# A graph layer with a mixture of experts on one core: expert results stored whole at their list rows, and gathered from there block by block

## The chip, the cores and the metric

The kernel runs on one core of a Trainium2 chip. The metric is the device time of one launch in microseconds; smaller is better. Three runs of the kernel before gave 1312.43, 1315.35 and 1317.46 us, with a median of 1315.35 us.

## The reference

There are 6250 nodes with 256 features, padded to 49 blocks of 128 nodes, and 100,000 edges. First a graph layer, then a layer of 8 experts of which each node uses two:

```python
x = x + gnn(layernorm(x)); x = x + ffn(layernorm(x))
# gnn: out = feat @ W_self + (segment_sum(feat[src], dst) / max(deg, 1)) @ W_neigh + b
# ffn: xn = layernorm(x) * gamma + beta;  logits = xn @ Wr + br
#      two best experts of a node, w = softmax(their logits)
#      h = gelu(xn @ W1[e] + b1[e]);  y_e = h @ W2[e] + b2[e]     (W1: 256x512, W2: 512x256)
#      y = y + y_e * w_full[..., e]
```

All of it is float32. The edges come sorted by `dst`.

## The kernel before, in words

**Slots.** Everything is laid out in slots `t`, numbered from 0 on. `plan` gives each step of each piece of work a slot, and every engine's program is a loop over the slots. The engines meet at semaphores alone.

**Edges.** In each of the slots 0 to 195 one group of 512 edges is worked off. GpSimd gathers their source rows from `feature_table` with four indirect DMAs (`gather`, L660) into `ring`, which holds four groups. GpSimd may therefore be at most about three groups ahead of TensorE. VectorE builds one-hot matrices (L1220), TensorE multiplies (`group`, L927, 8 rows of matmul in the trace per slot), and VectorE adds the sums to `agg` (L1274).

**Blocks.** As the edges of a block of 128 nodes are done, the block (called n, counted from the last block of nodes) goes through turns, products, normalization and the router. A routed block gets, for each node, two places in the lists of its experts (`slots`), and GpSimd scatters its rows twice into `expert_rows` (`scatter_rows`, L668).

**Dense blocks.** Blocks in `DENSE_BLOCKS`, nine of them (and the last block, 48), are not routed. They run through all eight experts, one *unit* per expert and block (`early_in`, hidden L1003 and result L1037), and VectorE adds each expert's share to `agg` (L1448, L1452). This fills the time before there are lists.

**Tiles.** Routed rows are worked off in 85 tiles of 128 rows of one expert's list. SyncE loads rows and weights (`load_rows`, `load_w1_of`), TensorE does hidden (L1003) and result (L1029), VectorE adds the bias and weighs (`weighted`, L1426, L1428). Then GpSimd puts the tile's rows with one indirect DMA into `node_rows`, which has two rows per node (`put_rows`, L679); the row number travels as an extra column of the list row. A tile is a unit too.

**Merges.** For each routed block SyncE loads the two rows of each node with one plain DMA (`load_pair`, L487), the two are added, the block's `x1` is added (L1409), and SyncE stores the block (`store_merged`, L493). 22 merges are done in slots 136 to 181, with two buffers, both additions on VectorE. They may start there because `merge_claim` proves from the counts that certain early blocks have all been handed out. The other 17 come at the end, behind the last tile. There GpSimd does the first addition (L686), ten buffers are used, and the second additions stand among the eight units of the last dense block on VectorE, three behind each `dense_sum`.

If a claim fails, all engines run the whole second half again, by a slow general path (`again`).

Of the kernel before, what the change touches and what calls it, by code (L numbers as in the profile page):

```python
# [6 lines left out]
P = 128  # L7
F32 = mybir.dt.float32
# [13 lines left out]
XP = 6  # L22
XR = 9
XW = 3
XY = 6
CONSTS = 20
EMPTY = 18
RAW = 4
DENSE_BLOCKS = (0, 3, 6, 9, 15, 21, 27, 33, 47)
DENSE_GAP = (1.25, 2.3)  # L30
MERGE_CLAIMS = ((28, 8), (32, 16), (36, 20), (40, 24), (44, 28))
MERGE_BUFFERS = 10
# [14 lines left out]
              "weigh": (5, 2), "add": (9, 5)}  # L47
# [5 lines left out]
def plan(NB, NG, NE):  # L53

# [78 lines left out]
def build(nc, x, src, dst, w_self, w_neigh, b_gnn, gamma, beta, w_r, b_r, w1, b1, w2, b2, out):  # L133
# [17 lines left out]
    merge_buffer = [i % 2 if at is not None else i % MERGE_BUFFERS for i, (n, c, at) in enumerate(merges)]  # L151
# [16 lines left out]
    node_rows = nc.dram_tensor("node_rows", [2 * NP + 3 * P, D], F32, kind="Internal").ap()  # L168
# [7 lines left out]
    with ExitStack() as ctx:  # L176
# [37 lines left out]
        node_i = sb("node_i", [P, NB, 2], I32)  # L214
# [6 lines left out]
        empty_row = sb("empty_row", [P, 3, R])  # L221
# [23 lines left out]
        slot_i = [sb(f"slot_i{s}", [P, 2], I32) for s in range(XP)]  # L245
# [43 lines left out]
        pair = sb("pair", [P, 2 * D])  # L289
        ring_flat = ring[:, :, :].rearrange("p a b -> p (a b)")  # L290
        merge_b = [dst_i[:, DK * P:DK * P + 2 * D].bitcast(F32), pair[:, :]]
        merge_b += [ring_flat[:, k * 2 * D:(k + 1) * 2 * D] for k in range(MERGE_BUFFERS - 2)]
        snap = sb("snap", [1, len(MERGE_CLAIMS), NE])
        late = sb("late", [1, len(MERGE_CLAIMS) + 1])
# [7 lines left out]
        small_in, dst_in, src_in, w2_in, b_in = (sem(n) for n in ("small_in", "dst_in", "src_in", "w2_in", "b_in"))  # L302
# [93 lines left out]
        merge_io = [(s, 16) for s in x_in] + [(sem(f"merge_io{k}"), 0) for k in range(MERGE_BUFFERS - len(x_in))]  # L396
# [38 lines left out]

        def dense_in(t):

            return [e for e in range(NE) if DENSE + e == t]
# [4 lines left out]
        def _(sp):  # L443
# [25 lines left out]
            sp.dma_start(out[NP:NP + P, :], empty_row[:, 0, 0:D]).then_inc(trash_out, 16)  # L469
# [67 lines left out]
            for t in range(END):  # L537
# [13 lines left out]
                for i in merges_in(t, 2):  # L551
                    load_pair(i)
# [1088 lines left out]
```

## Time and profile before

| | us |
|---|---|
| median of three runs | 1315.35 |
| time of the profiled execution | 1316.61 |
| its span in the trace | 1314.6 |
| TensorE matmul busy | 1155.8 |
| VectorE busy | 879.9 |
| ScalarE busy | 424.9 |
| GpSimd busy | 960.6 |

The mean granted clock of TensorE was 0.968. Times in the trace count from the start of the span. "Busy" for a GpSimd indirect DMA is the time in which GpSimd makes its descriptors; the transfer comes after. A short idle time stands ahead of each of these instructions, and the rows list it apart as idle released by "issue". A slot ends with its eight L927 matmuls, so slot borders can be read from them: slot 54 ends at 357 us, slot 136 at 884, slot 180 at 1177, slot 195 at 1264.

### The profile page before, as it was taken

To read this page: it belongs to the slowest core of one execution; us is meant where nothing else is said; L and a number is where in the kernel's file an instruction comes from. 1 tells how busy PE (TensorE), PEld (TensorE's weight loads), DVE (VectorE), ACT (ScalarE), POOL (GpSimd) and SP (SyncE) were. 2 spreads that over 40 slices of the span, in tenths; PEclk is the share of its full clock that TensorE was granted. 3 is DMA by queue.
4 is the path that set the end of the run, shared out by engine and by line. 5 is a ranking of instruction groups with operands and counts; after the bars stand their busy time and mean duration, and the time that the engine had idled before them with its cause. 6 is when DMAs were issued, how large, how long until landed. Compare 5 with 4: busy or idle time off the path is not lost.

```text
span 1314.6 us, 22817 instructions
## 1 busy us (share of the span) xinstructions
PE 1155.8 (88%) x6764; PEld 1030.2 (78%) x6765; DVE 879.9 (67%) x2835; ACT 424.9 (32%) x795; POOL 960.6 (73%) x1039
## 2 busy tenths in 40 slices
PE   0269999999988989999998999999888897999978
PEld 0248888888977879898897988988777795888867
DVE  6946666677677576877666677786587775664536
ACT  5503333323324333343342333343233331311121
POOL 6577777777767777777777777777777777777752
PEclk9978999999989999999998999999899998999989
DMA  9887765656655666666666756667557677677657
GB/s 334 263 259 226 221 194 178 189 168 197 206 165 171 200 193 209 189 210 205 197 221 185 214 183 191 204 212 245 178 168 228 224 235 237 224 236 219 222 165 233
DMA packets 154938, 276.16 MB, mean 210 GB/s; under 512 B 26464, under 2 KB 76896, under 8 KB 154688
## 3 DMA queue, kind: packets, MB, share of 16 engines
q1 hardware_dynamic: 103792, 142.94, 33.8%
q0 software_dynamic: 45456, 124.27, 30.9%
q10 hardware_dynamic: 5568, 7.47, 1.8%
q8 instruction: 59, 0.97, 0.3%
q14 instruction: 63, 0.52, 0.1%
HBM read 236.72 MB, written 37.86 MB: 209 GB/s over the span
## 4 chain that ended last, share of the span: by engine, by line
PE 73%; DVE 16%; issue 5%; DMA 2%; ACT 2%; POOL 1%; DVEq 1%; SPq 0%; ACTq 0%; POOLq 0%
PE bank L927 22%; PE bank L1003 19%; PE bank L1029 11%; PE bank L1037 9%; PE bank L915 3%; PE bank L956 3%; PE bank L958 3%; DVE heap L1417 2%; DVE agg L1274 2%; ACT heap L766 1%; DMA heap<-in_x 1%; PE bank L973 1%; DVE onehot L1220 1%; POOL ring L660 1%; PE bank L1053 1%
## 5 line engine op out<-in xcount | busy, mean ns | idle before, releaser
L660 POOL DMA_INDIRECT ring<-feature_table,src_sb x768 | 748.6, 975 | 252.5 <-issue 220.6
L927 PE MATMUL bank<-ring,onehot 128*128 128x257 f32 x1568 | 394.8, 396 | 84.8 <-DVE onehot L1220 52.6
L927 PEld LDWEIGHTS bank<-ring,onehot 128*128 128x128 f32 x1568 | 307.7, 199 | 140.4 <-issue 82.6
L1417 DVE TENSOR_TENSOR heap<-bank,b_sb 128x512 f32<-128x512 f32 x157 | 108.4, 691 | 224.7 <-PE bank L1003 83.5
L828 ACT ACTIVATE heap<-heap 128x512 f32<-128x512 f32 x157 | 98.9, 630 | 429.8 <-DVE heap L1417 429.8
L1029 PE MATMUL bank<-heap 128*128 x680 | 170.5, 395 | 18.4 <-DVE inside L1426 6.2
L1003 PE MATMUL bank<-row_t,heap 128*128 128x128 f32 x1360 | 166.8, 276 | 1.8 <-DVE heap L1417 1.8
L1003 PEld LDWEIGHTS bank<-row_t,heap 128*128 128x128 f32 x1360 | 161.1, 193 | 3.7 <-issue 2.6
L1029 PEld LDWEIGHTS bank<-heap 128*128 128x128 f32 x680 | 127.8, 196 | 36.9 <-issue 21.1
L1037 PE MATMUL bank<-heap 128*128 128x256 f32 x576 | 142.5, 391 | 15.8 <-DVE agg L1452 8.8
L1003 PE MATMUL bank<-dst_i,heap 128*128 128x128 f32 x1152 | 141.6, 276 | 0.6 <-DVE heap L1417 0.6
L1003 PEld LDWEIGHTS bank<-dst_i,heap 128*128 128x128 f32 x1152 | 137.9, 193 | 3.9 <-issue 1.6
L1274 DVE SCALAR_TENSOR_TENSOR agg<-bank,in_first,agg 128x257 f32 x196 | 94.2, 480 | 69.2 <-PE bank L927 44.2
L1220 DVE TENSOR_TENSOR onehot<-iota,target 128x512 f32<-128x512 f32 x196 | 134.4, 686 | 6.1 <-DVE xf L1291 5.0
L1037 PEld LDWEIGHTS bank<-heap 128*128 128x128 f32 x576 | 106.9, 193 | 30.6 <-issue 17.7
L821 ACT ACTIVATE row_t<-bank,gb_sb 128x128 f32<-128x128 f32 x170 | 68.4, 454 | 118.3 <-PE bank L915 118.2
L668 POOL DMA_INDIRECT expert_rows<-rows,slot_i x78 | 80.6, 1034 | 23.8 <-issue 23.8
L1274 DVE SCALAR_TENSOR_TENSOR agg<-bank,in_second,agg 128x257 f32 x196 | 93.2, 475 | 0.0
L788 ACT ACT_TABLE_LOAD x47 | 60.3, 1283 | 0.8
L956 PE MATMUL bank<-wn_sb,sums_t 128*128 128x256 f32 x196 | 53.8, 398 | 7.2 <-DVE logits L1324 6.4
L828 ACT ACT_TABLE_LOAD x46 | 59.0, 1283 | 0.8
L806 ACT ACTIVATE normal_t<-bank,gb_sb 128x128 f32<-128x128 f32 x80 | 32.1, 451 | 77.1 <-PE bank L915 77.1
(179 smaller groups left out, 1241.7 us busy)
## 6 DMA issues: line engine op xcount, KB each, us to landing
heap<-in_w SPq DMA_DIRECT2D x314, 256.0 KB
ring<-feature_table,src_sb POOLq DMA_INDIRECT x768
row<-expert_rows SPq DMA_DIRECT2D x85, 129.0 KB, 4.1
xf<-in_x SPq DMA_DIRECT2D x49, 128.0 KB
ff<-feature_table SPq DMA_DIRECT2D x49, 128.0 KB
feature_table<-heap SPq DMA_DIRECT2D x6, 896.0 KB, 5.7
heap<-in_w SPq DMA_DIRECT2D x4, 1024.0 KB, 5.7
heap<-in_w ACTq DMA_DIRECT2D x16, 256.0 KB
```

The lines of the kernel that those rows point to most:

```text
L660: pool.indirect_dma_start(ring[:, q * GT + i, 0:D], None, x if t < RAW else table, bass.IndirectOffsetOnAxis(src_sb[:, k:k + 1], 0)).then_ ...
L668: pool.indirect_dma_start(rows_tab, bass.IndirectOffsetOnAxis(slot_i[s][:, c:c + 1], 0), rows[s][:, c, :], None).then_inc(S.scattered[s], 16)
L821: last = act.activation(row_t[s][:, k, :], turned_b[:, k * P:(k + 1) * P], ACT.Identity, bias=gb_sb[:, 1, k:k + 1], scale=gb_sb[:, 0, k:k ...
L828: act.activation(hid[s], hid[s], ACT.Gelu).then_inc(S.gelu, 1)
L927: last = pe.matmul(bank[t % 2][:, 0:D + 1], onehot[:, q, i, :], ring[:, q * GT + i, :], start=(i == 0), stop=(i == GT - 1))
L956: pe.matmul(product_b[:, D:2 * D], t[:, k, :], wn_sb[:, k, :], start=(k == 0), stop=(k == DK - 1))
L1003: last = pe.matmul(hidden_b[:, c * P:(c + 1) * P], w1_of[w][:, k, c * P:(c + 1) * P], turned[:, k, :], start=(k == 0), stop=(k == DK - 1))
L1029: last = pe.matmul(result_b[:, 0:D], hid[s][:, k, :], w2_sb[:, k, bass.ds(e, 1), :].rearrange("p o d -> p (o d)"), start=(k == 0), stop=(k ...
L1037: last = pe.matmul(result_b[:, 0:D], hid[unit_of_dense[u] % 2][:, k, :], w2_sb[:, k, u % NE, :], start=(k == 0), stop=(k == HK - 1))
L1220: dve.tensor_tensor(onehot[:, q, :, :], iota[:, :].unsqueeze(1).broadcast_to([P, GT, P]), target[:, g * GT:(g + 1) * GT].unsqueeze(2).broa ...
L1274: last = dve.scalar_tensor_tensor(out=a, in0=bank[t % 2][:, 0:D + 1], scalar=mask[:, g:g + 1], in1=a, op0=ALU.mult, op1=ALU.add)
L1417: dve.tensor_tensor(hid[S.slot(u, 2)], hidden_b[:, :].rearrange("p (k t) -> p k t", k=HK), b1_sb[:, bass.ds(e, 1), :].rearrange("p o k -> ...
```

## The change

Three things are changed together.

1. **Results are stored whole.** `put_rows` on GpSimd is gone. SyncE stores the 128 rows of a tile with one plain DMA in `expert_out`, at the same place that its rows had in the lists (`store_rows`), two slots behind the weighing. The place of every node's two rows is now kept for all blocks (`slots_of`).
2. **Merges gather.** GpSimd gathers the rows of each node of a block with two indirect DMAs from `expert_out` into the two halves of a merge buffer (`take_rows`). It does so in the same slot in which VectorE adds both halves and `x1` (`add_rows`), with three buffers in the stage and eight at the end. SyncE no longer loads pairs, and GpSimd no longer adds.
3. **Seven dense blocks.** They are 0, 3, 6, 9, 18, 27 and 47, not 0, 3, 6, 9, 15, 21, 27, 33 and 47. There are then 56 dense units, not 72, and 89 tiles, not 85. 41 blocks are merged, not 39: 23 in slots 136 to 180 and 18 at the end.

An expert's share of the table is now 2176 rows on the planned path; if an expert has more than 2048 rows (`share_claim`), the slow path runs. SyncE also fills the whole of `expert_out` with zeros, in 68 DMAs of 256 rows of 1 KB each (17.8 MB), two in each of the slots 10 to 43.

```diff
-CONSTS = 20
+CONSTS = 16
+SHARE = 17 * P
-DENSE_BLOCKS = (0, 3, 6, 9, 15, 21, 27, 33, 47)
+DENSE_BLOCKS = (0, 3, 6, 9, 18, 27, 47)
-MERGE_CLAIMS = ((28, 8), (32, 16), (36, 20), (40, 24), (44, 28))
-MERGE_BUFFERS = 10
+MERGE_CLAIMS = ((28, 12), (32, 16), (36, 20), (40, 24), (44, 28))
+MERGE_BUFFERS = 8
+MERGE_SEMS = 4
+STAGE_BUFFERS = 3
...
-              "weigh": (5, 2), "add": (9, 5)}
+              "weigh": (5, 2), "store": (7, 4), "add": (9, 5)}
...
+    CAP = 3 * SHARE
+    FILLS = NE * SHARE // (2 * P)
...
-            def load_pair(i):
-                n, c, at = merges[i]
-                k = merge_buffer[i]
-                if k >= 2:
-                    sp.wait_ge(summed, NG)
-                io, base = merge_io[k]
-                sp.wait_ge(io, base + 32 * merge_use[i])
-                tiles_put(hold, main, lists[c][1])
-                b = NB - 1 - n
-                sp.dma_start(merge_b[k], node_rows[2 * P * b:2 * P * (b + 1), :].rearrange("(p c) d -> p (c d)", c=2)).then_inc(io, 16)
...
+            def store_rows(S, j):
+                if S.planned:
+                    tiles_put(hold, S, max(j - 1, 0))
+                else:
+                    hold(S.y_put[0], 16 * j)
+                hold(S.y_set, j + 1)
+                if S.planned and j == 0:
+                    sp.wait_ge(trash_out, 16 * (FILLS + EMPTY + 1))
+                at, = load_values(mybir.EngineType.SP, list_i[0:1, bass.ds(j, 1), 1], NE * CAP + (EMPTY - 1) * P, **unchecked)
+                sp.dma_start(expert_out[bass.ds(at, P), :], y_out[S.slot(j, XY)][:, :]).then_inc(S.y_put[S.slot(j, 2)], 16)
...
+                for i in range(FILLS):
+                    if t == 2 * HK + 2 + i // 2:
+                        two = expert_out[2 * P * i:2 * P * (i + 1), :].rearrange("(p c) d -> p c d", c=2)
+                        sp.dma_start(two, empty_row[:, 0:D].unsqueeze(1).broadcast_to([P, 2, D])).then_inc(trash_out, 16)
+                for j in tiles_in(t, "store"):
+                    store_rows(main, j)
                 for i in merges_in(t, -1):
                     store_merged(i)
-                for i in merges_in(t, 2):
-                    load_pair(i)
...
-            def put_rows(S, j):
-                if S.planned:
-                    tiles_put(hold, S, max(j - 1, 0))
-                else:
-                    hold(S.y_put[0], 16 * j)
-                hold(S.y_set, j + 1)
-                pool.indirect_dma_start(node_rows, bass.IndirectOffsetOnAxis(row[S.slot(j, XR)][:, D + 1:R].bitcast(I32), 0),
-                                        y_out[S.slot(j, XY)][:, :], None).then_inc(S.y_put[S.slot(j, 2)], 16)
-
-            def add_pair(i):
+            def take_rows(i):
+                n, of_list, at = merges[i]
                 k = merge_buffer[i]
-                io, base = merge_io[k]
-                pool.wait_ge(io, base + 32 * merge_use[i] + 16)
-                pool.tensor_tensor(merge_b[k][:, 0:D], merge_b[k][:, 0:D], merge_b[k][:, D:2 * D], ALU.add).then_inc(halved, 1)
+                if k >= STAGE_BUFFERS:
+                    pool.wait_ge(summed, NG)
+                pool.wait_ge(x_in[k], 16 * (merge_use[i] + 1))
+                pool.wait_ge(taken[i % MERGE_SEMS], 32 * (i // MERGE_SEMS))
+                tiles_put(hold, main, lists[of_list][1])
+                for c in range(2):
+                    pool.indirect_dma_start(merge_b[k][:, c * D:(c + 1) * D], None, expert_out[0:NE * SHARE, :],
+                                            bass.IndirectOffsetOnAxis(slots_at(main, n)[:, c:c + 1], 0)).then_inc(taken[i % MERGE_SEMS], 16)
...
                 for n in routed_in(t, "scatter"):
                     scatter_rows(main, n)
-                for j in tiles_in(t, "add"):
-                    put_rows(main, j)
+                for i in merges_in(t):
+                    take_rows(i)
             for i in range(STAGE_MERGES, len(merges)):
-                add_pair(i)
+                take_rows(i)
...
+            def add_rows(i):
                 k = merge_buffer[i]
-                io, base = merge_io[k]
-                dve.wait_ge(io, base + 32 * merge_use[i] + 16)
-                dve.tensor_tensor(merge_b[k][:, 0:D], merge_b[k][:, 0:D], merge_b[k][:, D:2 * D], ALU.add).then_inc(halved, 1)
+                m = merge_b[k]
+                after = linker(halved, i, 1)
+                dve.wait_ge(taken[i % MERGE_SEMS], 32 * (i // MERGE_SEMS + 1))
+                after(dve.tensor_tensor(m[:, 0:D], m[:, 0:D], m[:, D:2 * D], ALU.add))
+                dve.tensor_tensor(m[:, 0:D], m[:, 0:D], x1_of(main, merges[i][0]), ALU.add).then_inc(merged, 1)
```

The order of instructions shows where this lands. On GpSimd (POOL), from the first tiles on, in the kernel before; `node_rows` is where a put goes, `expert_rows` where a scatter goes, `ring` where a gather goes (x4 is one slot):

```order
L660 DMA ring<-feature_table,src_sb 128x256 x12
L668 DMA expert_rows<-rows2,slot_i2 53504x258 x2
L679 DMA node_rows<-inside,row1 12928x256
L660 DMA ring<-feature_table,src_sb 128x256 x8
L679 DMA node_rows<-inside,row2 12928x256
L660 DMA ring<-feature_table,src_sb 128x256 x4
L668 DMA expert_rows<-rows3,slot_i3 53504x258 x2
L679 DMA node_rows<-y_out3,row3 12928x256
```

And the same stretch of GpSimd after the change:

```order
L674 DMA ring<-feature_table,src_sb 128x256 x16
L682 DMA expert_rows<-rows2,slots_of 54528x257 x2
L674 DMA ring<-feature_table,src_sb 128x256 x12
L682 DMA expert_rows<-rows3,slots_of 54528x257 x2
L674 DMA ring<-feature_table,src_sb 128x256 x12
L682 DMA expert_rows<-rows4,slots_of 54528x257 x2
```

The puts are gone from between the gathers. Of the 85 puts, 38 stood in slots before 136, 35 in slots 136 to 180, 8 in slots 181 to 195 and 4 behind the last gather. In their place stand pairs of gathers from `expert_out`, 23 pairs in slots 136 to 180. The end of GpSimd's program in the kernel before, from the last gather of edges (here a put, then four, then the first additions of pairs):

```order
L660 DMA ring<-feature_table,src_sb 128x256 x4
L679 DMA node_rows<-y_out3,row0 12928x256
L679 DMA node_rows<-y_out4,row1 12928x256
L679 DMA node_rows<-y_out5,row2 12928x256
L679 DMA node_rows<-inside,row3 12928x256
L686 TENSOR_TENSOR ring<-ring 128x256 x8
L686 TENSOR_TENSOR dst_i<-dst_i 128x256
L686 TENSOR_TENSOR pair<-pair 128x256
L686 TENSOR_TENSOR ring<-ring 128x256 x7
```

And the end after the change, from the last pair in the stage on:

```order
L695 DMA pair0<-expert_out,slots_of 128x256 x2
L674 DMA ring<-feature_table,src_sb 128x256 x60
L695 DMA ring<-expert_out,slots_of 128x256 x2
L695 DMA dst_i<-expert_out,slots_of 128x256 x2
L695 DMA pair0<-expert_out,slots_of 128x256 x2
L695 DMA pair1<-expert_out,slots_of 128x256 x2
L695 DMA ring<-expert_out,slots_of 128x256 x10
L695 DMA dst_i<-expert_out,slots_of 128x256 x2
L695 DMA pair0<-expert_out,slots_of 128x256 x2
L695 DMA pair1<-expert_out,slots_of 128x256 x2
L695 DMA ring<-expert_out,slots_of 128x256 x10
L695 DMA dst_i<-expert_out,slots_of 128x256 x2
```

The last 15 slots now hold gathers of edges alone on GpSimd, and 36 gathers of result rows stand behind them, all of which wait for the last tile's store. On SyncE, in the first of the slots 10 to 43, after the change (`in_w1` are expert weights; the rows with `expert_out` are new):

```order
L562 DMA expert_rows<-empty_row 128x257
L566 DMA expert_out<-empty_row 256x1x256 x2
L517 DMA heap<-in_w1 128x512 x2
L562 DMA expert_rows<-empty_row 128x257
L566 DMA expert_out<-empty_row 256x1x256 x2
L488 DMA xf1<-in_x 128x256
L489 DMA ff1<-feature_table 128x256
```

The two zero fills of a slot stand ahead of the slot's loads of nodes and weights in the same queue.

## Rows read from the trace of the kernel before

**Rows 1.** The page, parts 1 and 4: engines busy; chain that ended last.
```profile
PE 1155.8 (88%) x6764; PEld 1030.2 (78%) x6765; DVE 879.9 (67%) x2835; ACT 424.9 (32%) x795; POOL 960.6 (73%) x1039
...
PE 73%; DVE 16%; issue 5%; DMA 2%; ACT 2%; POOL 1%; DVEq 1%; SPq 0%; ACTq 0%; POOLq 0%
```

**Rows 2.** Windows: start:end length, busy and count by engine, PEclk, DMA share, GB/s.
```profile
53.00:357.00 304.00, 270.99 (x1530) 239.94 (x1530) 205.57 (x663) 88.73 (x156) 226.20 (x232) 0.96 0.66 205
357.00:884.00 527.00, 500.14 (x3004) 450.70 (x3003) 371.69 (x1252) 189.63 (x350) 400.61 (x407) 0.98 0.63 197
884.00:1177.00 293.00, 259.69 (x1515) 229.73 (x1514) 193.25 (x616) 87.42 (x172) 222.14 (x225) 0.97 0.69 220
1177.00:1266.00 89.00, 83.80 (x503) 73.79 (x501) 43.74 (x90) 16.71 (x33) 66.27 (x68) 1.00 0.67 213
90.00:100.00 10.00, 4.26 (x11) 3.44 (x12) 1.66 (x4) 0.03 (x1) 7.57 (x9) 0.58 1.03 361
```

**Rows 3.** Groups of GpSimd instructions, window 357:884: busy, mean ns, idle before.
```profile
L660 POOL DMA_INDIRECT ring<-feature_table,src_sb x326 | 316.5, 971 | 102.0 <-issue 95.4 <-PE bank L927 3.8 <-DVE rows L1345 2.6
L668 POOL DMA_INDIRECT expert_rows<-rows,slot_i x42 | 44.3, 1055 | 12.8 <-issue 12.8
L679 POOL DMA_INDIRECT node_rows<-inside,row x21 | 21.6, 1030 | 6.4 <-issue 6.1 <-DVE rows L1345 0.3
L679 POOL DMA_INDIRECT node_rows<-y_out,row x18 | 18.3, 1019 | 5.5 <-issue 5.5
```

**Rows 4.** The same groups of GpSimd, window 884:1177.
```profile
L660 POOL DMA_INDIRECT ring<-feature_table,src_sb x171 | 168.0, 983 | 52.5 <-issue 47.2 <-PE bank L927 1.9 <-DVE inside L1428 1.2
L668 POOL DMA_INDIRECT expert_rows<-rows,slot_i x20 | 20.0, 998 | 6.1 <-issue 6.1
L679 POOL DMA_INDIRECT node_rows<-y_out,row x18 | 18.2, 1014 | 6.6 <-issue 5.2 <-DVE y_out L1428 1.4
L679 POOL DMA_INDIRECT node_rows<-inside,row x16 | 16.7, 1046 | 5.8 <-issue 4.3 <-DVE inside L1428 1.2 <-DVE y_out L1428 0.3
```

**Rows 5.** Waits of TensorE, window 1177:1266: engine, line, releaser, us, times, longest.
```profile
PE bank L927 <- issue: 5.1, 6, 2.0
```

**Rows 6.** The chain that ended last, from 1177: start, length, what.
```profile
1182.50 1.79 PE bank L1003 x16
1184.28 1.73 PE bank L1029 x8
...
1264.12 1.76 PE bank L1029 x8
```

**Rows 7.** Timeline of TensorE at slot 136: start, length, instructions.
```profile
882.35 1.90 PE L927 MATMUL bank<-ring,onehot 128*128 128x257 f32 x8
```

**Rows 8.** Timeline of GpSimd: the last gather of slot 136.
```profile
867.69 0.95 POOL L660 DMA_INDIRECT ring<-feature_table,src_sb  x1 [0.30 <-issue]
```

**Rows 9.** The page, part 3: packets, MB, share of 16 engines' span.
```profile
q1 hardware_dynamic: 103792, 142.94, 33.8%
```

**Rows 10.** Timeline, 86:101: the group of slot 10 and the gathers around.
```profile
88.34 0.95 POOL L660 DMA_INDIRECT ring<-feature_table,src_sb  x1 [0.30 <-issue]
95.74 3.77 PE L927 MATMUL bank<-ring,onehot 128*128 128x257 f32 x8 [6.86 <-issue]
```

**Rows 11.** Puts (L679) in the whole trace: the row on landing.
```profile
DMA to landing us min/median/max: 2.4/2.5/5.5
```

**Rows 12.** Timeline, 1262:1275: last tile weighed, put, and first pair load.
```profile
1266.57 0.35 DVE L1428 TENSOR_SCALAR inside<-inside,row 128x256 f32<-128x256 f32 x1
1267.73 0.97 POOL L679 DMA_INDIRECT node_rows<-inside,row  x1 [2.52 <-DVE inside L1428]
1270.29 3.27 SPq L487 DMA_DIRECT2D ring<-node_rows  x7
```

**Rows 13.** Timeline, 1303:1316: the last steps of all.
```profile
1306.19 1.01 DVE L1409 TENSOR_TENSOR ring<-ring,agg 128x256 f32<-128x256 f32 x2
1311.14 0.33 SPq L583 DMA_DIRECT2D out<-agg  x1
```

More of the change, by code:

```diff
@@ L150, in build @@
     UNITS = EARLY + NJ
-    merge_buffer = [i % 2 if at is not None else i % MERGE_BUFFERS for i, (n, c, at) in enumerate(merges)]
+    merge_buffer = [i % STAGE_BUFFERS if at is not None else i % MERGE_BUFFERS for i, (n, c, at) in enumerate(merges)]
     merge_use = [merge_buffer[:i].count(merge_buffer[i]) for i in range(len(merges))]
@@ L394, in build @@
         halved, merged = sem("halved"), sem("merged")
-        merge_io = [(s, 16) for s in x_in] + [(sem(f"merge_io{k}"), 0) for k in range(MERGE_BUFFERS - len(x_in))]
+        taken = [sem(f"taken{k}") for k in range(MERGE_SEMS)]
+        assert len(x_in) >= MERGE_BUFFERS
         LAST = NB - 1
@@ L507, in close_lists @@
                     ends = load_values(mybir.EngineType.SP, end_i[0:1, e0:e0 + 4], NE * CAP - P, **unchecked)
-                    for e, end in enumerate(ends):
-                        sp.dma_start(rows_tab[bass.ds(end, P), :], empty_row[:, e % 2, :]).then_inc(S.ends_out, 16)
+                    for end in ends:
+                        sp.dma_start(rows_tab[bass.ds(end, P), :], empty_row[:, :]).then_inc(S.ends_out, 16)
                 sp.wait_ge(S.ends_out, 16 * NE)
@@ L592, in _ @@
                 sp.wait_ge(edges_done, 1)
+                for i in range(EMPTY):
+                    sp.dma_start(rows_tab[NE * CAP + i * P:NE * CAP + (i + 1) * P, :], empty_row[:, :]).then_inc(trash_out, 16)
                 load_nodes(again, 0, 0)
@@ L723, in _, with take_again @@
                     scatter_rows(again, n)
-                put_rows(again, 0)
-                with pool.Fori(1, NJ_ALL) as j:
-                    put_rows(again, j)
                 pool.wait_ge(again.y_put[0], 16 * NJ_ALL)
+                def take_again(n):
+                    hold(edges_done, n * 16 + 1)
+                    pool.tensor_copy(slot_2[:, :], slots_of[:, bass.ds(NB - 1 - n, 1), :].rearrange("p o c -> p (o c)")).then_inc(m_idx, 1)
+                    hold(m_idx, n + (NT + 1))
+                    for c in range(2):
+                        pool.indirect_dma_start(again_b[:, c * D:(c + 1) * D], None, expert_out,
+                                                bass.IndirectOffsetOnAxis(slot_2[:, c:c + 1], 0)).then_inc(m_gathered, 16)
+                take_again(0)
+                with pool.Fori(1, NB) as n:
+                    take_again(n)
         @block.scalar
```

116 lines of the change are left out of this document (56 added, 60 removed).

## The prediction, made before the changed kernel ran

> **What bounds the kernel now.** I read the page first, then windows, then the groups of GpSimd, then waits, the chain and the timeline. The page gives TensorE 88% of the span, GpSimd 73%, VectorE 67%, and the chain that ended last lies 73% on TensorE [rows 1]. That reads as a TensorE bound, and it is half the truth. From slot 54 to slot 136 (357 to 884 us) TensorE is busy for 500.1 of 527 us [rows 2]. In the same stretch GpSimd's groups with the short idle ahead of each come to 316.5 + 102.0 (gathers), 44.3 + 12.8 (scatters) and 39.9 + 11.9 (puts), together 527.4 us [rows 3]. GpSimd is full too. The plan has balanced both. What decides which one is late is GpSimd's lead: the last gather of slot 136 ends at 868.6, its group starts at 882.4, 13.7 us later [rows 7, 8]. So here TensorE sets the pace. From 884 to 1177 GpSimd comes to 220.5 + 26.1 + 24.8 + 22.5 = 293.9 of 293 us [rows 4], and TensorE is idle for 33 [rows 2]: here GpSimd sets it. From 1177 to 1266 TensorE is idle for 5.2 us, of which 5.1 are waits of the group in six slots, with no engine named as releaser, which is how a gather that isn't there yet looks [rows 2, 5]. The end, 1265.9 to 1314.6, is 48.7 us of the last dense block and 17 merges [rows 6].
>
> **Slots 54 to 135.** A unit costs TensorE 1.79 + 1.73 = 3.52 us [rows 6]. Before slot 136 there are 104 units now and 92 after the change: 12 x 3.52 = 42.2 us less, with about 1 us more for the turns of two more tiles and the places of two more routed blocks: -41. GpSimd loses 38 puts of 51.8/39 = 1.33 us and gets 4 scatters of 57.1/42 = 1.36 us: -50.5 + 5.4 = -45 [rows 3]. The gain is the smaller of both, as both are full: -41 (0 if neither followed, -45 at most). VectorE, 371.7 of 527 us busy [rows 2], loses work as well and doesn't come into it.
>
> **Slots 136 to 180.** 35 puts go, 46 gathers of result rows come. A put costs 47.3/34 = 1.39 us here, a gather 220.5/171 = 1.29 [rows 4]: -48.7 + 59.3 = +10.7 on the engine that sets the pace. TensorE has 38 units before and after. The value taken is +11; it is 0 if the 13.7 us of lead swallow it, but stage one takes as much from GpSimd as from TensorE, so I expect no larger lead at slot 136 than now, rather a smaller one, since the missing dense units are not spread evenly.
>
> A new wait stands here. GpSimd takes a merge's rows behind the gathers of the same slot at whose end VectorE waits for them. Before, SyncE had loaded them two slots ahead. Behind VectorE's wait are queued the next one-hots, the next bias, and so the gelu and the result. VectorE has 293 - 193 = 100 us idle in this stretch [rows 2], and a late bias in a stretch in which TensorE waits for gathers anyway costs little. I take +2; the bounds are 0 and 12, half a microsecond for each of 23 merges.
>
> **SyncE's stores** are put at nothing. What hides them is that a store of a tile waits for the weighing of two slots earlier, while the weights and rows issued behind it are for two slots later. If that cover were gone, a unit would wait for its weights; the bound is 0 to 3, and it goes into the range.
>
> **Slots 181 to 195.** 8 puts go, no gather comes: GpSimd has 8 x 1.39 = 11 us less. TensorE gains only its waits for gathers, -5 [rows 5]. It is the bound then.
>
> **The zero fills.** 17.8 MB is new on SyncE's queue. That queue moved 142.94 MB in 33.8% of the 16 engines' span [rows 9], so 17.8 MB is 4.2%, or 55 us of all 16 engines, within the 200 us or so of slots 10 to 43. It lifts a DMA share of 0.66 [rows 2] to about 0.93. Mostly it fits. It doesn't where SyncE issues several slots' work at once: in 90 to 100 us the share is 1.03 already [rows 2], and the group of slot 10 starts at 95.74, 6.4 us after its last gather was made, with TensorE idle for 6.86 and the granted clock at 0.58 in that window, between its levels of 1.2 and 2.4 GHz [rows 2, 10]. About ten fills (2.6 MB, 7 us at 361 GB/s) come on top. I take +4, between 0 (all hidden, as GpSimd is ahead afterwards) and 7 for the burst; a rival below has the rest.
> By the Trainium skill ("DMA: Bandwidth & Descriptors", SWDGE vs HWDGE vs iDMA) each DMA engine takes turns between the queues of GpSimd and of SyncE. Fills would then not stand ahead of gathers, and the term would be near 0. The trace agrees with it only in part: with the engines full, a gather started at 88.34 kept its group waiting until 95.74, 7.4 us, where a put lands 2.5 us after its start [rows 10, 11].
>
> **The end.** Now the last tile's result ends at 1265.9 [rows 6], it is weighed by 1266.9, put from 1267.7, and the first pair load is issued at 1270.3, 4.4 us after the result [rows 12]. A plain store should be no slower, so 4.4 stays. Then 18 merges x 2 = 36 gathers go one after the other on GpSimd, since all wait for the last store: 36 x 1.29 = 46.4 us (45.0 at the 0.95 + 0.30 of a quiet one [rows 8], 50.0 at the price of a put). The last lands 1.5 us after its descriptors are made (2.5 from its start for a put, up to 5.5 [rows 11]). The rest is the chain that there is: two additions, bias, gelu, result, sum, store, from 1306.2 to 1314.6 = 8.4 us [rows 13], because the last three merges stand behind the sixth expert's sum on VectorE, ahead of the last bias. That is 4.4 + 46.4 + 1.5 + 8.4 = 60.7 us where 48.7 are now: +12 (10.5 to 18.6). Eight buffers don't limit it: one comes round after 8 x 2.6 = 21 us. The dense units, 3.5 us each, fall from bound to hidden.
>
> **Sum.** -41 + 11 + 2 - 5 + 4 + 12 = -17 us, on the profiled execution's 1316.6: 1299 us. That execution lay 1.3 us above the median of 1315.35, within the spread of the runs, so the forecast is 1299. Its own range is 1289 to 1309.
>
> **Rivals.**
> *GpSimd's lead carries over* (1281). If stage one leaves GpSimd its 13.7 us of lead, the +11 vanishes, the waits of VectorE too, and fills and end cost 0 and 10.5: -41 - 5 + 10.5 = -35.5. For it: the lead is full again and again now. Against it: GpSimd's own work fills the 293 us of slots 136 to 180 even now [rows 4], and TensorE is idle for 33 of them.
> *The gains meet each other* (1315). Both engines are full, but not in the same slots; with gathers at 5.2 us per slot as a floor and dense units missing in clumps, stage one gives 30, not 41. With +11, +4 for VectorE's waits, -5, +4 and an end at +15 the sum is -1. For it: 527.4 of 527 us on GpSimd [rows 3].
> *The fills stand on the path* (1332, slower). Of their 55 us two thirds (37) are paid, 33 more than I count: weights and gathers come late in slots 10 to 43, where TensorE has 271 of 304 us busy [rows 2] and no reserve, and the clock falls at each idle spell. It decides from 27 us on: above that the kernel is slower than before by over 0.5%. Against it: the share would be 0.93, not over 1.
> *The change doesn't run its planned path.* If an expert had over 2048 rows or a claim failed, the second half would be done again by the slow path, far above any time here. The reference's routing gives 1613 rows for the fullest expert over the 41 routed blocks, so I give it 1 in 50.
>
> **Numbers.** Forecast 0.50, lead carries over 0.13, gains meet 0.20, fills 0.15, slow path 0.02. A measurement of this kernel can tell about 0.5% from no change, so faster is below 1308.8 and slower above 1321.9. Faster 0.50 + 0.13 = 0.63; same 0.21 (gains meet, and a little of the forecast's edge); slower 0.16. The range 1281 to 1322 leaves out most of the fills and the slow path.
>
> **What would show it.** Slot 54 ends at 357 to 362 us (fills). Slot 136 ends near 847. In slots 136 to 180 the span is about 306 us, not 293, and TensorE's waits for the group grow. Slots 181 to 195 show no such wait. The last tile's result ends near 1237, GpSimd then runs 36 gathers without a break, and 61 us follow. I would be wrong if slot 54 ends over 15 us later than now, if GpSimd has gaps in the end, or if stage one gives under 30 us.

## The result, and the profile after

| | before | after |
|---|---|---|
| median of 4 runs, us | 1315.68 (1312.43 to 1317.46) | 1303.37 (1302.63 to 1304.21) |
| ratio to before, 95% interval | | 0.9909 (0.9889 to 0.9930) |
| profiled execution, its span, us | 1316.6, 1314.6 | 1303.35, 1301.4 |

The change makes the kernel 12.3 us (0.9%) faster; 1299 was forecast, with 1289 to 1309 as the forecast's own range. The page after, parts 1, 3 and 4, beside [rows 1, 9]:

```profile
PE 1120.8 (86%) x6492; PEld 998.0 (77%) x6493; DVE 867.2 (67%) x2789; ACT 422.4 (32%) x793; POOL 946.3 (73%) x1019
...
q1 hardware_dynamic: 126608, 156.39, 36.7%
...
PE 63%; DVE 15%; issue 7%; DMA 6%; POOL 5%; SPq 2%; ACT 2%; DVEq 1%; POOLq 0%; ACTq 0%
```

TensorE lost 272 matmuls and 35.0 us of work, and only 13.2 us of the span went. Where the other 22 are can't be read here, but the chain hints at it: it lies 10 points less on TensorE, and GpSimd, DMA and "issue" took them. The windows of the changed kernel, cut at the ends of its own slots 54, 136 and 180 and at the last tile's result (1237), beside [rows 2]:

```profile
53.00:357.00 304.00, 268.50 (x1537) 238.17 (x1536) 206.14 (x656) 88.78 (x156) 227.19 (x232) 0.96 0.82 265
357.00:842.00 485.00, 457.06 (x2733) 411.56 (x2732) 353.08 (x1197) 186.87 (x347) 359.50 (x366) 0.98 0.65 198
842.00:1154.00 312.00, 264.48 (x1503) 232.73 (x1502) 193.09 (x610) 87.62 (x173) 237.90 (x244) 0.93 0.70 215
1154.00:1237.00 83.00, 82.80 (x508) 75.32 (x507) 44.32 (x92) 16.73 (x33) 56.00 (x57) 1.00 0.74 227
1237.00:1301.00 64.00, 44.09 (x212) 37.43 (x210) 32.47 (x84) 10.78 (x16) 35.22 (x36) 0.77 0.52 159
```

Cutting both traces at the ends of the same slots' groups of eight matmuls gives this account (us; the last cut is the end of slot 195):

| stage | before | after | difference | forecast |
|---|---|---|---|---|
| to slot 54 | 356.9 | 356.4 | -0.5 | +4 |
| slots 55 to 136 | 527.4 | 485.8 | -41.6 | -41 |
| slots 137 to 180 | 292.3 | 312.2 | +19.9 | +11, and +2 of waits |
| slots 181 to 195 | 87.5 | 81.2 | -6.3 | -5 |
| from there to the end | 50.5 | 65.8 | +15.3 | +12 |
| span | 1314.6 | 1301.4 | -13.2 | -17 |

Two terms hold, slots 55 to 136 and 181 to 195; the fills cost nothing; the third and the fifth were too small. The third stage shows why. GpSimd's groups from 842 to 1154, beside [rows 4]:

```profile
L674 POOL DMA_INDIRECT ring<-feature_table,src_sb x180 | 176.1, 978 | 54.9 <-issue 52.8 <-PE bank L946 1.2 <-DVE rows L1365 0.3
L695 POOL DMA_INDIRECT pair<-expert_out,slots_of x30 | 29.0, 968 | 9.1 <-issue 8.8 <-DMA expert_out<-inside 0.3
L682 POOL DMA_INDIRECT expert_rows<-rows,slots_of x20 | 20.0, 1001 | 6.1 <-issue 5.8 <-DMA expert_out<-y_out 0.3
L695 POOL DMA_INDIRECT dst_i<-expert_out,slots_of x14 | 13.9, 990 | 4.3 <-issue 3.7 <-DMA expert_out<-inside 0.3 <-DMA expert_out<-y_out 0.3
```

They come to 313.4 of 312 us: GpSimd is full and sets the pace, as forecast. 44 gathers of result rows (56.3 us with their idle time) stand where 34 puts stood (47.3), which is +9.0. The gathers of edges are 180 where they were 171 [rows 4], and that is the part I had not counted: 9 x 1.28 = 11.5 us. The stage has 44 slots and needs 176 gathers of edges in either kernel. Before, five of them were made ahead of the stage, in GpSimd's lead (the time from the end of a slot's last gather to the end of its group); now GpSimd makes them all there, and four for the next stage. The timeline around the group of slot 136, beside [rows 7, 8] (first GpSimd's last gather for it, then TensorE's group):

```profile
835.18 0.95 POOL L674 DMA_INDIRECT ring<-feature_table,src_sb  x1 [0.30 <-issue]
...
840.32 1.90 PE L946 MATMUL bank<-ring,onehot 128*128 128x257 f32 x8
```

From the end of the last gather to the end of the group it is 842.2 - 836.1 = 6.1 us, where it was 15.6. At slot 125 the lead was still 17.9 us (16.8 before). It goes in the eleven slots between, because no dense unit is left there: GpSimd makes 34 gathers of edges in that time, where eleven slots use up 44. The work on `heap` by TensorE in those slots, before (816.6 to 884.3):

```profile
L1029 PE MATMUL bank<-heap 128*128 x40 | 9.8, 389 | 0.8 <-DVE y_out L1426 0.8
L1037 PE MATMUL bank<-heap 128*128 128x256 f32 x40 | 9.8, 387 | 0.0
L1003 PE MATMUL bank<-row_t,heap 128*128 128x128 f32 x80 | 9.7, 275 | 0.0
L1003 PE MATMUL bank<-dst_i,heap 128*128 128x128 f32 x80 | 9.7, 275 | 0.0
```

And after (787.7 to 842.2):

```profile
L1022 PE MATMUL bank<-row_t,heap 128*128 128x128 f32 x96 | 11.7, 275 | 0.0
L1048 PE MATMUL bank<-heap 128*128 x48 | 11.6, 384 | 0.0
```

Five dense units (80 / 16, on `dst_i`) are gone, and one of routed work more is there (96 / 16 for 80 / 16). TensorE now needs 54.5 / 11 = 4.95 us per slot, less than the four gathers alone (4 x 1.25 = 5.0), and eats 12 us of lead. It is no loss in that stage, it is one in the next, where GpSimd is still full and what TensorE ran ahead is paid back. TensorE's waits for the group of a slot in slots 137 to 180 show it, before and after (releaser, us, times, longest):

```profile
PE bank L927 <- issue: 8.6, 8, 4.5
```

```profile
PE bank L946 <- issue: 19.9, 7, 7.2
```

From 1154 to 1237 that wait is gone, beside the 5.1 us of [rows 5]:

```profile
PE bank L946 <- issue: 0.2, 1, 0.2
```

The end, beside [rows 12, 13]: the last tile's result, its store, the first, a middle and the last gathers of result rows, and the last steps of all.

```profile
1235.70 1.67 PE L1048 MATMUL bank<-heap 128*128 x7
1238.08 0.35 DVE L1450 TENSOR_SCALAR y_out<-y_out,row 128x256 f32<-128x256 f32 x1
1238.97 0.33 SPq L547 DMA_DIRECT2D expert_out<-y_out  x1
1241.56 0.95 POOL L695 DMA_INDIRECT ring<-expert_out,slots_of  x1 [14.49 <-DMA expert_out<-y_out]
...
1263.33 0.97 POOL L695 DMA_INDIRECT ring<-expert_out,slots_of  x1 [1.67 <-issue]
...
1287.90 0.95 POOL L695 DMA_INDIRECT dst_i<-expert_out,slots_of  x1 [0.30 <-issue]
1290.74 0.42 DVE L1430 TENSOR_TENSOR dst_i<-dst_i 128x256 f32<-128x256 f32 x1 [1.66 <-DMA dst_i<-expert_out,slots_of]
1292.94 3.78 PE L1083 MATMUL bank<-heap 128*128 128x256 f32 x8 [3.76 <-ACT heap L863]
1296.83 0.48 DVE L1493 SCALAR_TENSOR_TENSOR agg<-bank,spread,agg 128x256 f32<-128x256 f32 x1 [3.17 <-PE bank L1083]
1297.34 0.33 SPq L598 DMA_DIRECT2D out<-agg  x1
```

The result is there at 1237.4 and the first gather starts 4.2 us later (forecast 4.4). The 36 gathers take 1241.56 to 1288.85 = 47.3 us (forecast 46.4), with one idle time of 1.67 ahead of the first gather into a buffer used for the second time, 1.4 more than the usual 0.30. The last rows land 1.9 us after their descriptors (forecast 1.5). What then follows takes 1301.4 - 1290.7 = 10.7 us and not 8.4: the last eight matmuls take 3.78 us, where the chain that ended last has for the kernel before

```profile
1308.52 2.01 PE bank L1064 x8
```

The windows around these matmuls, in the changed kernel and in the kernel before:

```profile
1291.00:1301.00 10.00, 3.78 (x8) 2.52 (x8) 3.04 (x7) 0.63 (x1) 0.00 (x0) 0.56 0.10 30
```

```profile
1305.00:1311.00 6.00, 4.12 (x18) 2.87 (x16) 4.51 (x10) 1.26 (x2) 1.07 (x2) 1.00 0.31 105
```

The mean granted clock is 0.56 of full (2.4 GHz) in the first, so for most of it the lower level of 1.2 GHz was granted, and TensorE had been idle for 3.76 us ahead of these eight. In the second it is 1.00, and the idle time ahead of the eight was 0.45 us. In sum 64.0 us from the last result, where 48.7 was the time before and 60.7 the forecast.

### The profile page after: what moved, and what is told of

Same layout as the page of the kernel before. It is cut to its first block, busy times and chain, and to the rows that moved or that the text cites. A ratio compares the mean times of both kernels' runs of the same rounds, so it can differ in the third digit from the quotient of the medians.

```text
span 1301.4 us, 22560 instructions
## 1 busy us (share of the span) xinstructions
PE 1120.8 (86%) x6492; PEld 998.0 (77%) x6493; DVE 867.2 (67%) x2789; ACT 422.4 (32%) x793; POOL 946.3 (73%) x1019
## 4 chain that ended last, share of the span: by engine, by line
PE 63%; DVE 15%; issue 7%; DMA 6%; POOL 5%; SPq 2%; ACT 2%; DVEq 1%; POOLq 0%; ACTq 0%
PE bank L946 19%; PE bank L1022 16%; PE bank L1048 9%; PE bank L1056 7%; POOL ring L674 3%; PE bank L934 3%; PE bank L975 3%; PE bank L977 3%; DVE agg L1293 2%; DVE heap L1439 1%; ACT heap L785 1%; DMA expert_out<-inside 1%; DMA heap<-in_x 1%; PE bank L992 1%; DMA expert_out<-y_out 1%
## 5 line engine op out<-in xcount | busy, mean ns | idle before, releaser
L1439 DVE TENSOR_TENSOR heap<-bank,b_sb 128x512 f32<-128x512 f32 x145 | 100.0, 690 | 184.3 <-PE bank L1022 85.0
L847 ACT ACTIVATE heap<-heap 128x512 f32<-128x512 f32 x145 | 91.3, 630 | 367.3 <-DVE heap L1439 367.1
L1048 PE MATMUL bank<-heap 128*128 x712 | 177.2, 393 | 20.0 <-DVE y_out L1448 9.6
L1022 PE MATMUL bank<-row_t,heap 128*128 128x128 f32 x1424 | 178.4, 280 | 0.0
L1022 PEld LDWEIGHTS bank<-row_t,heap 128*128 128x128 f32 x1424 | 172.7, 197 | 1.3
L1048 PEld LDWEIGHTS bank<-heap 128*128 128x128 f32 x712 | 133.3, 195 | 38.4 <-issue 22.1
L1293 DVE SCALAR_TENSOR_TENSOR agg<-bank,in_first,agg 128x257 f32 x196 | 94.2, 481 | 77.4 <-PE bank L946 46.4
L1056 PE MATMUL bank<-heap 128*128 128x256 f32 x448 | 110.1, 389 | 10.4 <-DVE agg L1474 8.8
L1022 PE MATMUL bank<-dst_i,heap 128*128 128x128 f32 x896 | 109.5, 275 | 0.9 <-DVE heap L1439 0.9
L1022 PEld LDWEIGHTS bank<-dst_i,heap 128*128 128x128 f32 x896 | 106.4, 192 | 3.5 <-issue 1.7
L682 POOL DMA_INDIRECT expert_rows<-rows,slots_of x82 | 82.9, 1011 | 25.0 <-issue 24.7
L1056 PEld LDWEIGHTS bank<-heap 128*128 128x128 f32 x448 | 82.8, 193 | 21.9 <-issue 12.2
```

Of the source, the lines that this page charges most:

```text
L682: pool.indirect_dma_start(rows_tab, bass.IndirectOffsetOnAxis(slots_at(S, n)[:, c:c + 1], 0), rows[s][:, c, :], None).then_inc(S.scattered ...
L847: act.activation(hid[s], hid[s], ACT.Gelu).then_inc(S.gelu, 1)
L1022: last = pe.matmul(hidden_b[:, c * P:(c + 1) * P], w1_of[w][:, k, c * P:(c + 1) * P], turned[:, k, :], start=(k == 0), stop=(k == DK - 1))
L1048: last = pe.matmul(result_b[:, 0:D], hid[s][:, k, :], w2_sb[:, k, bass.ds(e, 1), :].rearrange("p o d -> p (o d)"), start=(k == 0), stop=(k ...
L1056: last = pe.matmul(result_b[:, 0:D], hid[unit_of_dense[u] % 2][:, k, :], w2_sb[:, k, u % NE, :], start=(k == 0), stop=(k == HK - 1))
L1293: last = dve.scalar_tensor_tensor(out=a, in0=bank[t % 2][:, 0:D + 1], scalar=mask[:, g:g + 1], in1=a, op0=ALU.mult, op1=ALU.add)
```

## Experiments

Each kernel was run beside the kernel before on the same chip. The first four shared one chip (before: 1315.36, n = 19).

**Storing and gathering alone.** Nine dense blocks, as before.

```diff
-DENSE_BLOCKS = (0, 3, 6, 9, 18, 27, 47)
+DENSE_BLOCKS = (0, 3, 6, 9, 15, 21, 27, 33, 47)
```

> The changed kernel with the nine dense blocks of before, so storing whole and gathering alone. Theory (GpSimd and TensorE are both full in slots 54 to 135, and what counts is the later of the two): TensorE has all its 104 units again, so slot 136 ends near 880 us, within 10 us of the kernel before, although GpSimd has 38 puts less. GpSimd then stands at full lead (14 to 18 us) there, the extra gathers of slots 136 to 180 cost 0 to 9 us, slots 181 to 195 give 5, the end costs 15 more. Total 1313 to 1328 us, so no gain over before. Rival (GpSimd alone is the bound): slot 136 ends 40 us earlier even so, and the total is below 1300.

Measured 1318.74 (n = 10), ratio 1.0031 (1.0004 to 1.0058): no gain, as expected. Slot 136 ends at 878.1 (884.3 before). The last gather of its slot and its group:

```profile
857.52 0.94 POOL L674 DMA_INDIRECT ring<-feature_table,src_sb  x1 [0.31 <-issue]
...
876.19 1.90 PE L946 MATMUL bank<-ring,onehot 128*128 128x257 f32 x8
```

GpSimd's lead is 19.6 us: freed of 38 puts it only waits for TensorE. Storing and gathering by itself wins 6 us up to slot 136, and loses 7.6 in slots 137 to 180 (299.9 for 292.3) and 9.6 behind slot 195 (60.1 for 50.5); 6 us come back in slots 181 to 195 (81.4 for 87.5).

**Seven dense blocks alone**, in the kernel before.

```diff
-DENSE_BLOCKS = (0, 3, 6, 9, 15, 21, 27, 33, 47)
+DENSE_BLOCKS = (0, 3, 6, 9, 18, 27, 47)
```

> The kernel before with the seven dense blocks, puts and pair loads kept, so the fewer dense units alone. Theory (both are full): GpSimd keeps its puts and gets 4 scatters and 4 puts more, so slot 136 ends 0 to 10 us earlier than before, with no lead left on GpSimd there and TensorE waiting for gathers; slots 136 to 180 are not shorter than 293 us; the end stays at 49 us. Total 1308 to 1325 us. Rival (TensorE alone is the bound, as its 88% and the chain say): slot 136 ends 35 us or more earlier, total near 1280.

Measured 1321.78 (n = 10), ratio 1.0060 (1.0038 to 1.0081). Slot 136 ends at 882.2:

```profile
876.55 0.95 POOL L660 DMA_INDIRECT ring<-feature_table,src_sb  x1 [0.30 <-issue]
...
880.32 1.90 PE L927 MATMUL bank<-ring,onehot 128*128 128x257 f32 x8
```

The lead is 4.7 us: now GpSimd holds TensorE back, which has lost its 12 units for nothing. Slots 55 to 136 take 525.9 us here and 521.8 with storing and gathering alone, where they took 527.4, and 485.8 with both. So the reading that both engines are full there [rows 2, 3] is shown. Over the whole kernel each half is slower by itself (+3 and +6 us), both together are 12 us faster.

This run also shows what the lead is worth. It has puts as before and not one gather of result rows, and slots 137 to 180 take 302.9 us for 292.3. In them GpSimd's gathers of edges, beside [rows 4]'s 171, and TensorE's waits for a group, beside the 8.6 us above, are:

```profile
L660 POOL DMA_INDIRECT ring<-feature_table,src_sb x179 | 175.3, 979 | 54.6 <-issue 50.6 <-DVE rows L1345 1.2 <-DVE inside L1428 0.9
```

```profile
PE bank L927 <- issue: 27.1, 13, 7.2
```

With storing and gathering alone, where the lead at slot 136 was kept (19.6 us), the same stage lost 7.6 us, which is the exchange of puts for gathers. The two losses, 10.6 and 7.6, come to 18.2 of the 19.9 us of the changed kernel.

**The additions one slot later.** VectorE adds a merge, and SyncE stores it, one slot after GpSimd gathered it.

```diff
-                for i in merges_in(t, -1):
+                for i in merges_in(t, -2):
...
-                for i in merges_in(t):
+                for i in merges_in(t, -1):
```

> The changed kernel with each merge in the stage added and stored one slot later than its rows are gathered, so that VectorE doesn't wait for the gather of its own slot; all else is the same. Theory (slots 136 to 180 grew by 20 us because GpSimd has more to do and no lead to spend): VectorE's waits for gathered rows (some 20 us in the trace) shrink to nearly nothing, but the total falls by 0 to 3 us, to 1300 to 1303. Rival (VectorE's wait holds up the bias and so TensorE): slots 136 to 180 get 8 to 12 us shorter and the total is 1291 to 1295.

Measured 1301.23 (1298.56 to 1301.85), ratio 0.9889 (0.9862 to 0.9917). VectorE's waits for gathered rows between 842 and 1154 in the changed kernel were these, and in this one there is none in those slots:

```profile
DVE pair L1430 <- DMA pair<-expert_out,slots_of: 12.7, 4, 5.2
...
DVE dst_i L1430 <- DMA dst_i<-expert_out,slots_of: 4.3, 2, 4.0
```

17.0 us of waits went and some 2 us of time with them. That fits the forecast's +2, but its interval and that of the changed kernel overlap, and slots 137 to 180 (308.7 us here, 312.2 there) also took 308 us in another kernel below in which nothing of them was changed. So these waits are cheap, at most 2 to 4 us; more isn't shown.

**Each fill twice**, 35.6 MB of zeros in the same slots.

```diff
-    FILLS = NE * SHARE // (2 * P)
+    FILLS = 2 * NE * SHARE // (2 * P)
...
-                    if t == 2 * HK + 2 + i // 2:
-                        two = expert_out[2 * P * i:2 * P * (i + 1), :].rearrange("(p c) d -> p c d", c=2)
+                    if t == 2 * HK + 2 + i // 4:
+                        h = i % (FILLS // 2)
+                        two = expert_out[2 * P * h:2 * P * (h + 1), :].rearrange("(p c) d -> p c d", c=2)
```

> The changed kernel with every zero fill done twice, four in each of the slots 10 to 43, so 17.8 MB more on SyncE's queue. Theory (the DMA engines had room, so the fills are free): the second round lifts the DMA share there to about 1.1 of what there is, so this overloads, and slot 54 ends 5 to 20 us later; that the first round cost nothing means that room of some 25% was there. Total 1306 to 1320. Rival (fills stand only in SyncE's own queue and never hold up a gather): slot 54 ends within 3 us of 356, total 1303.

Measured 1304.42 (1301.14 to 1308.45), ratio 0.9904 (0.9873 to 0.9934). The windows 88 to 220 of the kernel before, the changed one and this one:

```profile
88.00:220.00 132.00, 117.02 (x665) 104.00 (x664) 84.16 (x246) 35.84 (x60) 99.86 (x105) 0.94 0.70 216
```

```profile
88.00:220.00 132.00, 116.24 (x674) 103.06 (x672) 84.63 (x244) 36.71 (x63) 100.60 (x104) 0.96 0.95 309
```

```profile
88.00:220.00 132.00, 113.97 (x641) 99.48 (x640) 82.62 (x241) 36.73 (x62) 97.70 (x101) 0.96 1.06 379
```

At a DMA share of 0.95 TensorE does as much as at 0.70 (116.2 and 117.0 us of work). At 1.06 it does 2.3 us less, and slot 54 ends at 361.4, 5 us later; in the seven other kernels traced on chips of this speed it ends between 355.7 and 357.5. One filling is free, the second costs about 5 us, which the whole time doesn't show beyond its scatter.

**On chips that keep another time.** Six kernels ran on two other chips, on which the kernel before took 1632 and 1628 us, so their microseconds can't be set beside the rest. The changed kernel itself did not run on either.

Half the gathers, at the end (the condition shown) or in the stage (`i < STAGE_MERGES`). The second row of each node of these blocks is left out; the semaphore counts, not shown, follow:

```diff
+        def one_row(i):
+            return i >= STAGE_MERGES
...
-                for c in range(2):
+                for c in range(1 if one_row(i) else 2):
...
+                o = 0 if one_row(i) else D
+                after(dve.tensor_tensor(m[:, 0:D], m[:, 0:D], m[:, o:o + D], ALU.add))
```

> The changed kernel with only the first of a node's two rows gathered for the 18 merges at the end, so 18 gathers behind the last store, not 36; the result of those blocks is left incomplete. All waits and additions are the same. Theory (36 gathers one after the other on GpSimd set the end): from the last tile's result to the end 64 us become 44 to 50, where the eight units of the last dense block take over as bound, and the total is 1284 to 1290. Rival (landing of the transfers, buffers coming round or SyncE's stores set it): the end stays over 58 us, total over 1297.

Measured 1556.45, ratio 0.9554 (0.9456 to 0.9652).

> The changed kernel with only the first row gathered for the 23 merges in slots 136 to 180, so 23 gathers there, not 46; the result of those blocks is left incomplete. Theory (GpSimd's own work sets slots 136 to 180): 23 x 1.28 = 29 us less on GpSimd; slots 136 to 180 take 284 to 295 us, not 312, less than the full 29 because TensorE then becomes the bound; total 1283 to 1294. Rival (the growth there comes from waits of VectorE for rows that land late, not from GpSimd's load): at most 5 us less, total over 1298.

Measured 1557.07, ratio 0.9579 (0.9480 to 0.9677). The last claim moved up, alone and with the additions one slot later:

```diff
-MERGE_CLAIMS = ((28, 12), (32, 16), (36, 20), (40, 24), (44, 28))
+MERGE_CLAIMS = ((28, 12), (32, 16), (36, 20), (40, 24), (44, 36))
```

> The changed kernel with the last claim stretched from block 28 to block 36, which its counts allow: seven merges move from behind the last tile into slots 182 to 194. Theory (GpSimd has room in slots 181 to 195, where TensorE is the bound, and none at the end): 14 gathers of 1.28 us = 18 us go into a stretch with 8 to 15 us of idle and lead; it grows by 0 to 5 us. The end loses 14 x 1.26 = 18 us, down to 46 to 50. Total 1287 to 1294. Rival (the end is bound elsewhere, or the stretch has no room): total 1300 or more.

Measured 1584.74, ratio 0.9716 (0.9615 to 0.9817).

> The same with each merge in the stage added and stored one slot later than its rows are gathered. Theory: VectorE's waits for rows of its own slot cost 2 us of 1303 and are saved here too, 1285 to 1292. Rival (with the additions later, buffers and stores come late in the denser stretch): the same time as the claim alone, or 2 us more.

Measured 1596.22, ratio 0.9822 (0.9714 to 0.9931). The later additions make the claim's kernel 11 us slower here (1590.15 to 1604.84 for 1574.69 to 1587.01); the expectation's rival had at most 2, and why is not shown. Two more were run after these, half the gathers of the stage again, and the later additions with the last claim at (44, 32):

> The changed kernel, in which the 23 merges of slots 136 to 180 gather one result row in place of two (23 gathers fewer on GpSimd there; the sum then counts one row twice, so these result rows are incomplete). Theory (in these slots GpSimd's instructions set the pace, and each gather of result rows costs its full 1.25 to 1.29 us): slots 136 to 180 take 312.2 - 22 to 29 = 283 to 290 us, TensorE's idle time there falls from 47 to 18 to 25 us, and the whole is 1274 to 1283 us. Rival (the extra 20 us are VectorE's and TensorE's waits for rows that come late, not GpSimd's time): the rows are as late as before, slots 136 to 180 take 302 to 310 us, and the whole is 1293 to 1302 us.

Measured 1560.11, ratio 0.9646 (0.9553 to 0.9738).

> The changed kernel with the last claim moved from block 28 to block 32, so that four merges (8 gathers) go from the end into slots 182 to 188, and with each staged merge added and stored one slot later than it is gathered. Theory (GpSimd has 6 to 8 us of room in slots 181 to 195, which seven moved merges overran and four nearly fit; the end falls by 8 x 1.3 = 10 us towards the floor of some 50 us that the dense units set; the later additions give 2 us): slots 180 to 195 take 83 to 87 us (81.2 in the changed kernel), the end 53 to 56 us (64.0), the whole 1292 to 1298 us. Rival (no room in that stretch at all, as every gather on a full GpSimd costs its time wherever it stands): slots 180 to 195 take 90 to 92 us, and the whole is 1300 to 1303 us.

Measured 1591.46, ratio 0.9840 (0.9747 to 0.9934). On these chips the engines wait otherwise. The longest wait of VectorE in the second run with half the staged gathers ("remote": ended by another core or a queue that the profile doesn't know):

```profile
DVE heap L1448 <- remote: 234.0, 52, 12.3
```

In the traces of the chips with 1315 us no such row stands. TensorE is busy for 77% of the span, GpSimd for 60%, and GpSimd's lead is 24 to 27 us at the ends of slots 54, 136 and 180. No expected time was met, and neither of two theories about microseconds can be called right or wrong by them. Nor do they settle the price of a gather in the stage. On one chip the kernel with 23 gathers fewer takes 1375.9 - 1013.2 = 362.7 us for slots 137 to 180, the one with the later claim, which also adds later, 1422.6 - 1027.5 = 395.1: 32 us, or 1.4 us for each gather. On the other chip two kernels differ in that stage in the 23 gathers alone, half the gathers in the stage (369.0 us) and half at the end (385.7): 17 us, or 0.7 us for each. GpSimd is not full on these chips, so both numbers say little of the chips on which it is. Whether a claim up to block 32 beats the changed kernel where that one takes 1303 us stays open.

**Half the gathers at the end**, again, on a chip where the kernel before takes 1315.67. The edit is the one shown above.

> The kernel of tailhalf again, on another chip, since on the chip of the first run the kernel before took 1632 us, not 1315, and the end can't be read in the same terms. It gathers only the first of a node's two rows for the 18 merges at the end. Theory as before (the 36 gathers set the end): 64 us become 44 to 50, total 1284 to 1290. Rival (landing, buffers or stores set it): the end stays over 58 us, total over 1297.

Measured 1289.40 (1284.98 to 1293.56), ratio 0.9794 (0.9761 to 0.9828), 14 us under the changed kernel. GpSimd's eighth and ninth gather of the end, and VectorE's first addition:

```profile
1252.59 0.95 POOL L703 DMA_INDIRECT ring<-expert_out,slots_of  x1 [0.30 <-issue]
1263.74 0.94 POOL L703 DMA_INDIRECT ring<-expert_out,slots_of  x1 [10.20 <-issue]
```

```profile
1259.85 0.41 DVE L1439 TENSOR_TENSOR ring<-ring 128x256 f32<-128x256 f32 x1
```

It waits 10.20 us for a buffer: VectorE adds the first rows only at 1259.85, behind a step of the dense chain, and they must be stored first. From the last result to the end it is 50.5 us, where it was 64.0. The chain that ended last has no gather and no DMA among its 55 longest pieces from 1240 on; 48% of it are the matmuls of the dense units (L1080 25.8%, L1091 21.8%). So the last dense block is the floor there, and the gathers above it cost 13.5 us.

**The last claim up to block 36.** Seven merges (14 gathers) go from the end into slots 182 to 194, again beside 1315.67; the edit stands above.

> The kernel of claims36 again, on another chip: the last claim reaches block 36, and seven merges move from behind the last tile into slots 182 to 194. Theory: that stretch grows by 0 to 5 us, the end falls by 18 to 46 to 50 us, total 1287 to 1294. Rival (no room in the stretch, or the end is bound elsewhere): total 1300 or more.

Measured 1302.40 (1298.76 to 1304.70), ratio 0.9907 (0.9890 to 0.9923): no gain over the changed kernel. The window of slots 181 to 195, and TensorE's waits in it:

```profile
1151.00:1246.00 95.00, 83.69 (x501) 73.11 (x501) 49.28 (x104) 16.71 (x33) 68.50 (x72) 1.00 0.73 227
```

```profile
PE bank L946 <- issue: 11.2, 9, 2.3
```

The end fell from 64.0 to 49.1 us, as in the experiment before. The stage took 94.7 us, not 81.2. Counting GpSimd's idle time overstates the room: 56.0 us busy and 17 us of short idle in 83 leave 10 us, but they all lie behind its last gather. GpSimd makes its gathers of the stage without a pause in either kernel. The last of slot 195, first in the changed kernel and then in this one, with this one's group:

```profile
1226.12 0.94 POOL L674 DMA_INDIRECT ring<-feature_table,src_sb  x1 [0.31 <-issue]
```

```profile
1240.18 0.95 POOL L674 DMA_INDIRECT ring<-feature_table,src_sb  x1 [0.30 <-issue]
...
1243.95 1.98 PE L946 MATMUL bank<-ring,onehot 128*128 128x257 f32 x8 [0.69 <-issue]
```

The lead at slot 195 is 8.6 us in the changed kernel and 4.8 here (4.3 in the kernel before), so 3.8 us of the 17.5 us of gathers were taken in, and 13.7 were left; the stage grew by 13.5. What the end wins the stage loses.

## Why the prediction was right, step by step

- *Slots 54 to 135, -41.* Measured -41.6. That the gain is the smaller of both engines' is shown from both sides by the two halves of the change (-5.6 and -1.5 us in that stage).
- *Slots 136 to 180, +11 and +2.* The step that was mis-sized: +19.9. The exchange itself was priced about right (+9.0 for 44 gathers against 34 puts). What failed is the end of the step, "I expect no larger lead at slot 136 than now, rather a smaller one, since the missing dense units are not spread evenly": it names the cause and gives it no price. At slot 136 the lead fell from 15.6 to 6.1 us; at slot 180 it is 7.2 (5.3 before). So the kernel before spent 10.4 us of lead in the stage, and the changed one gained 1.1: 11.5 us, the price of the nine gathers. Fewer dense units alone, with no exchange at all, cost 10.6 us there. It could have been worked out: 171 gathers of edges in a stage that needs 176 [rows 4], the 13.7 us of [rows 7, 8], and the dense units of the last eleven slots, five of which went.
- *VectorE's waits, +2.* In line with the additions one slot later (2 us), not separated from scatter.
- *SyncE's stores, 0.* Not tested by itself. VectorE's waits for an earlier tile's store, in 842 to 1154, are longer than the 0.5 us that it waited for puts before:

```profile
DVE y_out L1448 <- DMA expert_out<-y_out: 3.8, 4, 1.3
DVE y_out L1448 <- DMA expert_out<-inside: 2.9, 1, 2.9
```

They lie in a stage in which GpSimd sets the pace, so a cost of nothing agrees with them and isn't shown.
- *Slots 181 to 195, -5.* Measured -6.3, the waits of the group gone (0.2 us).
- *The fills, +4.* Measured -0.5 to slot 54. The burst at slot 10 hardly came on top: the group's wait was 7.10 where it was [rows 10]'s 6.86, and the group ended at 100.8 for 99.5:

```profile
97.08 3.77 PE L946 MATMUL bank<-ring,onehot 128*128 128x257 f32 x8 [7.10 <-issue]
```

By the Trainium skill ("DMA: Bandwidth & Descriptors", SWDGE vs HWDGE vs iDMA), each DMA engine takes turns between the two kinds of queue, so that fills don't stand ahead of gathers. By that rule the term is near 0, as measured; with the doubled fills, at a share over 1, there is a cost of 5 us that the rule by itself doesn't give.
- *The end, +12.* Measured +15.3, from the last result. The start (4.2 for 4.4) was right. The gathers were 0.9 us over (47.3 for 46.4), with the 1.4 us for a buffer that "Eight buffers don't limit it" had ruled out; a gap in the end was named as a sign of being wrong, and this small one came. The landing was 0.4 us longer and the last steps 2.3 (10.7 for 8.4), of which 1.8 are matmuls at the lower clock.

Of the rivals, "the lead carries over" is the reverse of what happened. "The gains meet each other" was right in its cause, units missing in clumps, and in its +15 for the end, and wrong on the place: stage one gave the whole 41 us, and the next stage paid. "The fills stand on the path", 37 us, is refuted by the end of slot 54, 0.5 us earlier than before, and even twice the fills cost only 5. My errors were of opposite sign (fills -4.5, slots 55 to 136 and 181 to 195 -1.9, stage and end +10.2), which is why the sum came within 4 us. That much of it is luck.

## What to carry to other kernels

Where two engines are both full, taking work off one alone gave 2 to 6 us of 527 here, and taking it off both gave 42; look for a change that relieves both and price it by the smaller. Then carry the lead of the feeding engine over each border of a stage as a term of its own: the same stage costs more when the one before it hands over an empty ring. And before moving work out of a serial tail into an earlier stretch, take the room of that stretch from the feeding engine's lead at its end, not from its idle time: here it was 4 us and not 10.

## What the runs showed that was not expected

- A kernel of one core took 1315 us on some chips and 1628 to 1632 on two others, with about the same duration of a gather (969 to 977 ns there, 974 to 982 here) and 234 to 298 us of VectorE's waits on one line without a releaser on the core; GpSimd and ScalarE have such waits too. The granted clock was 0.89 to 0.92 there and 0.95 to 0.97 here. The ratios to the kernel before differ as well (0.972 for the claim up to block 36, where the other chip gave 0.991). What the chips differ in is not shown.
- The DMA engines took 17.8 MB more in 34 slots, to a share of 0.95 and 309 GB/s, without a measurable delay; at 1.06 and 379 GB/s the delay was 5 us.
